# Three 16x8-head attention layers of a 12-layer decoder: first jobs, loads, splits and staging rearranged

## The reference, cut to what matters

```
h = layernorm(x)                      # per token, over 128 channels
q = (h @ Wq + bq) * scale             # the self layer has no q/k/v biases
k = src @ Wk + bk ; v = src @ Wv + bv # src: context (512 x 96), or h (256 x 128)
p = softmax(q_head @ k_head.T)        # 16 heads; L0 clamps the scores at 1e4
x = x + concat(p @ v_head) @ Wo + bo  # L3 regroups the heads before Wo
```

## Time and profile before

| | us |
|---|---|
| median of 3 executions | 2374.45 (2373.88 to 2378.79) |
| the profiled execution | 2378.78, its span 2377.0 |
| PE busy | 2000.3 (84% of the span) |
| PE weight load busy | 1195.5 (50%) |
| DVE busy | 1440.6 (61%) |
| ACT busy | 1108.8 (47%) |
| POOL busy | 647.4 (27%) |
| HBM | 46 GB/s over the span |

### The profile page before, as it was taken

The page is one execution under the profiler, slowest core; times in us unless marked ns, Lnnn a source line. Parts: engine busy times, 40 slices in busy tenths (PEclk is TensorE's granted clock), DMA queues, the critical chain, the costliest instruction groups (busy, mean ns, idle before and its releaser), DMA issues. The chain is left out here.

```text
span 2377.0 us, 37476 instructions
## 1 busy us (share of the span) xinstructions
PE 2000.3 (84%) x12495; PEld 1195.5 (50%) x12495; DVE 1440.6 (61%) x3369; ACT 1108.8 (47%) x2808; POOL 647.4 (27%) x907
## 2 busy tenths in 40 slices
PE   6679999879995887666999996656899999599997
PEld 3434544434442554544666664435566666244444
DVE  6468899444433554684777765562666665477762
ACT  4325555534431665333555553220566666167762
POOL 7434342100003432101111105301434432333312
PEclk9769999889995888887999998865999999689996
DMA  1133321386642330001000001101000000434321
GB/s 34 30 95 70 76 51 42 74 189 144 143 99 69 80 77 19 23 0 37 1 2 1 2 2 31 33 1 42 1 2 2 1 2 1 105 77 86 76 48 26
DMA packets 126321, 112.29 MB, mean 47 GB/s; under 512 B 61193, under 2 KB 98996, under 8 KB 123828
## 3 DMA queue, kind: packets, MB, share of 16 engines
q1 hardware_dynamic: 92852, 108.84, 19.8%
q10 hardware_dynamic: 33280, 1.05, 0.7%
HBM read 93.67 MB, written 15.20 MB: 46 GB/s over the span
## 5 line engine op out<-in xcount | busy, mean ns | idle before, releaser
L957 DVE TENSOR_REDUCE L_xattn_mx<-L_xattn_psS 128x1 f32<-128x512 f32 x512 | 326.2, 683 | 116.1 <-PE L_xattn_psS L1082 112.1
L1192 ACT ACTIVATE L_xattn_PT<-L_xattn_psT 128x512 f32<-128x512 f32 x512 | 283.2, 600 | 95.1 <-PE L_xattn_psT L1094 89.5
L603 ACT ACTIVATE L_attn_pr<-L_attn_psS,L_attn_negm 128x256 f32<-128x256 f32 (+1 forms) x512 | 222.0, 446 | 103.1 <-DVE L_attn_negm L403 68.0
L1082 PE MATMUL L_xattn_psS<-L_xattn_KR,L_xattn_QR 72*128 72x512 bf16 x512 | 212.8, 421 | 43.2 <-DVE L_xattn_mx L957 21.1
L401 DVE TENSOR_REDUCE L_attn_mx<-L_attn_psS 128x2 f32<-128x512 f32 x256 | 164.9, 686 | 114.3 <-PE L_attn_psS L512 114.2
L1094 PE MATMUL L_xattn_psT<-L_xattn_QR,L_xattn_KR 75*128 75x256 bf16 x1024 | 198.3, 279 | 3.8 <-ACT L_xattn_PT L1192 1.6
L1108 PE MATMUL L_xattn_psO<-L_xattn_PT,L_xattn_V 128*32 128x256 f32 x2048 | 193.1, 400 | 3.2 <-ACT L_xattn_PT L1192 1.1
L2068 DVE TENSOR_TENSOR L_ffn_act<-L_ffn_act,L_ffn_cwb 128x512 f32<-128x512 f32 x128 | 86.7, 690 | 129.9 <-ACT L_ffn_act L2198 106.0
L512 PE MATMUL L_attn_psS<-L_attn_qk 64*128 64x256 f32 x1024 | 146.6, 404 | 11.6 <-ACT L_attn_pr L603 11.6
L2133 PE MATMUL L_ffn_psU<-L_ffn_hT,L_ffn_wup 128*128 128x512 f32 x256 | 133.3, 612 | 13.6 <-ACT L_ffn_act L2198 13.6
L2198 ACT ACTIVATE L_ffn_act<-L_ffn_psU 128x512 f32<-128x512 f32 (+1 forms) x132 | 78.5, 597 | 135.7 <-PE L_ffn_psU L2133 131.8
(11 more groups left out here) (553 smaller groups left out, 3952.1 us busy)
## 6 DMA issues: line engine op xcount, KB each, us to landing
L_ffn_cwb<-L_ffn_weights_by_expert SPq DMA_DIRECT2D x64, 512.0 KB, 7.8
L_xattn_KR<-L_xattn_k_parts SPq DMA_DIRECT2D x96, 192.0 KB
L_xattn_QR<-L_xattn_q_parts SPq DMA_DIRECT2D x32, 288.0 KB
L_xattn_k_parts<-L_xattn_ks SPq DMA_DIRECT2D x48, 128.0 KB, 2.4
L_xattn_ctxT<-in_ctx SPq DMA_DIRECT2D x24, 192.0 KB, 2.4
L_attn_QR<-L_attn_q_parts SPq DMA_DIRECT2D x16, 288.0 KB
L_attn_KR<-L_attn_k_parts SPq DMA_DIRECT2D x48, 96.0 KB
L_xattn_q_parts<-L_xattn_qs SPq DMA_DIRECT2D x48, 64.0 KB, 2.1
```

Source lines behind the costliest of these rows:

```text
L603: ins = nc.scalar.activation(pr[n % 3][:, r, t, 0:width], psS[(2 * n + r) % 3][:, t, 0:width], ACT.Exp, bias=negm[:, n % 4, t, r:r + 1], s ...
L957: nc.vector.reduce_max(mx[:, b % 2, u, hd:hd + 1], psS[n % 2][:], AX.X).then_inc(s_used, 1)
L1082: ins = nc.tensor.matmul(psS[n % 2][:, i * keys:(i + 1) * keys], QR[b % NB][0:PAIR, hd, t * P:(t + 1) * P], KR[b % NB][0:PAIR, hd, :], sta ...
L1192: nc.scalar.activation(PT[n % NPT][:, 2 * u:2 * u + 2], psT[i % NPS][:], ACT.Exp).then_inc(exp_ready, 1)
```

## The change

All in layer_attention_heads8, but for one packed input.

- First jobs: T, Q and K of batch 0 write to banks of their own (psT[0], psT[1], psS[0]) and don't wait for psM; the reads follow.
- Loads: the biases bq and bk are packed into two more columns of the query weight (made on the host), so that qk_loaded counts two DMAs; wv is loaded before bv, both behind the query weight; the ones rows are loaded behind spread 0, and POOL makes the ones tile behind the second norm.
- Cross layers: V of batch 0 moves from step FIRST to FIRST + 1 (ahead of K of batch 1, behind the first scores); DVE_SPLITS 2 becomes 1.
- Two buffers each for qs and ks, with a staging semaphore each; ACT, splits and spreads wait for the batch two before.
- Self layer: EARLY 6 becomes 4, APART 7 becomes 9, BACK 8 becomes 9; T, Q, K, V at 0, 4, 6, 8. T, Q, K, V of batch 1 are then at -17, -13, -11, -9 (before -17, -15, -13, -11), of batch 2 at -8, -4, -2, 0 (before -10, -8, -6, -4), of batch 3 at 1, 5, 7, 9 (before -3, -1, 1, 3); modulo 16 later: M 7, A 9, O 10, T 12, M 15, Q 0, K 2, V 4. SP's order becomes stage 0, spread 0, ones rows, stage 1, spread 1, rows(0,0), rows(0,1), stage 2, spread 2, rows(1,0), stage 3, spread 3, rows(1,1), and as before from there.
- LAST: two empty steps fewer in L0, one step more in the self layer.

```
-    LEAD, PREP, STAGE, EARLY, DVE_SPLITS = (HH + 6, 38, 7, 3, 2) if from_ctx else (HH + 10, 52, 9, 6, 3)
+    LEAD, PREP, STAGE, EARLY, DVE_SPLITS = (HH + 6, 38, 7, 3, 1) if from_ctx else (HH + 10, 52, 9, 4, 3)
-    APART, BACK = (4, 6) if from_ctx else (7, 8)
+    APART, BACK = (4, 6) if from_ctx else (9, 9)
-    FIRST, LAST = -LEAD, NH + (16 if head_major else 10)
+    FIRST, LAST = -LEAD, NH + (16 if head_major else BACK + 2)
-        for i, kind in ((0, "K"), (2, "T"), (3, "Q")) if from_ctx else ((0, "T"), (2, "Q"), (4, "K")):
+        for i, kind in ((0, "K"), (2, "T"), (3, "Q")) if from_ctx else ((0, "T"), (4, "Q"), (6, "K")):
-        jobs[max(H * b - LATE_V, FIRST) if from_ctx else at + 6 * (b > 0)].append(("V", b, 0))
+        jobs[max(H * b - LATE_V, FIRST + 1) if from_ctx else at + 8 * (b > 0)].append(("V", b, 0))
-        qs, ks = sb("qs", [P, PARTS, S], BF16), sb("ks", [P, PARTS, keys], BF16)
+        qs, ks = ([sb(f"{n}{i}", [P, PARTS, w], BF16) for i in range(2)] for n, w in (("qs", S), ("ks", keys)))
+        q_staged, k_staged = ([sem(f"{v}_staged{i}") for i in range(2)] for v in "qk")
-        WQK, WV = (4, 2) if bq is not None else (2, 1)
+        WQK, WV = (2, 2) if bq is not None else (2, 1)
+        def bank_of(job):
+            kind, b, _ = job
+            if b == 0 and kind in "TQ":
+                return psT["TQ".index(kind)][:].rearrange("p k s -> p (k s)")
+            return psS[0][:] if b == 0 and kind == "K" else psM[:]
-            loads = [(wk_s[:], m.dram[wk], qk_loaded), (wq_s[:], m.dram[wq], qk_loaded)]
+            loads = [(wk_s[:], m.dram[wk], qk_loaded), (wqb[:], m.dram[wq if bq is None else f"{pre}_q_pack"], qk_loaded), (wv_s[:], m.dram[wv], v_loaded)]
             if bq is not None:
-                loads += [(bk_s[:], ...), (bq_s[:], ...), (bv_s[:], ...)]
-            loads += [(wv_s[:], m.dram[wv], v_loaded), (wo_s[:], ...), (bo_s[:], ...)]
+                loads += [(bv_s[:], rows(m.dram[bv]).to_broadcast((P, D)), v_loaded)]
+            loads += [ (wo_s[:], ...), (bo_s[:], ...)]
-            sp.wait_ge(ones_set, 1)
-            for i in range(NB):
-                sp.dma_start(KR[i][PAIR:PAIR + PARTS], ones[:]).then_inc(rows_set, 16)
+            def one_rows():
+                sp.wait_ge(ones_set, 1)
+                for i in range(NB):
+                    sp.dma_start(KR[i][PAIR:PAIR + PARTS], ones[:]).then_inc(rows_set, 16)
...
                     if kind == "spread":
                         spread(b)
+                        if b == 0:
+                            one_rows()
...
             link(nc.gpsimd.memset(eps[:], LN_EPS))
-            nc.gpsimd.memset(ones[:], 1.0).then_inc(ones_set, 1)
             norm(0)
+            pool.wait_ge(h_ready, TB)
             nc.gpsimd.memset(V[0][:], 1.0).then_inc(v_set, 1)
             norm(1)
+            pool.wait_ge(h_ready, 2 * TB)
+            nc.gpsimd.memset(ones[:], 1.0).then_inc(ones_set, 1)
...
-                wait(pe, psM_read, place[job])
+                bank = bank_of(job)
+                if not (b == 0 and kind in "TQK"):
+                    wait(pe, psM_read, place[job])
...
-                    wait(act, staged, 16 * PARTS * b)
-                    nc.scalar.activation(parts[:, 0], psM[:, 0:width], ACT.Identity, bias=add, scale=by).then_inc(psM_read, 1)
+                    wait(act, staged, 16 * PARTS * (b // 2))
+                    nc.scalar.activation(parts[:, 0], bank_of(job)[:, 0:width], ACT.Identity, bias=add, scale=by).then_inc(psM_read, 1)
```

More of the change, by code:

```diff
@@ L698, in layer_attention_heads8 @@
         sb, ps, sem = allocators(nc, es, pre)
-        wq_s, wk_s, wv_s, wo_s = sb("wq", [P, D]), sb("wk", [CK, D]), sb("wv", [CK, D]), sb("wo", [P, D])
-        bq_s, bk_s = sb("bq", [P, 1]), sb("bk", [P, 1])
+        wqb, wk_s, wv_s, wo_s = sb("wq", [P, D + 2 * (bq is not None)]), sb("wk", [CK, D]), sb("wv", [CK, D]), sb("wo", [P, D])
+        wq_s = wqb[:, 0:D]
+        bq_s, bk_s = (wqb[:, D + i:D + i + 1] if bq is not None else None for i in range(2))
         bv_s, bo_s = sb("bv", [P, D]), sb("bo", [P, D])
@@ L803, in spread_k @@
                 def spread_k(heads, done):
[L804 removed]
+                    sp.wait_ge(k_staged[b % 2], 16 * PARTS * (b // 2 + 1))
                     for i in range(PARTS):
@@ L855, in split_q @@
             eng.wait_ge(q_high, b + 1)
-            wait(eng, q_staged, 16 * PARTS * b)
-            split(eng, link, qf, qs, q_split)
+            wait(eng, q_staged[b % 2], 16 * PARTS * (b // 2))
+            split(eng, link, qf, qs[b % 2], q_split)
         def split_k(eng, link, b):
             eng.wait_ge(k_high, b + 1)
-            wait(eng, k_staged, 16 * PARTS * b)
-            split(eng, link, kf, ks, k_split)
+            wait(eng, k_staged[b % 2], 16 * PARTS * (b // 2))
+            split(eng, link, kf, ks[b % 2], k_split)
         @block.gpsimd
@@ L1050, in run @@
                     pe.wait_ge(o_loaded, 16 * 2)
-                wait(pe, psM_read, place[job])
+                bank = bank_of(job)
+                if not (b == 0 and kind in "TQK"):
+                    wait(pe, psM_read, place[job])
                 if kind == "Q":
-                    ins = nc.tensor.matmul(psM[:, 0:S], wq_s[:], hT[:], start=True, stop=True)
+                    ins = nc.tensor.matmul(bank[:, 0:S], wq_s, hT[:], start=True, stop=True)
                 elif kind == "K":
-                    ins = nc.tensor.matmul(psM[:, 0:keys], wk_s[:], kv_source(b), start=True, stop=True)
+                    ins = nc.tensor.matmul(bank[:, 0:keys], wk_s[:], kv_source(b), start=True, stop=True)
                 elif kind == "V":
@@ L1066, in run @@
                     for t in range(TB):
-                        ins = nc.tensor.transpose(psM[:, t * P:(t + 1) * P], h[:, t], m.ident[:])
+                        ins = nc.tensor.transpose(bank[:, t * P:(t + 1) * P], h[:, t], m.ident[:])
                 else:
@@ L1144, in read @@
                 if kind == "T":
-                    nc.scalar.copy(hT[:], psM[:, 0:S]).then_inc(psM_read, 1)
+                    nc.scalar.copy(hT[:], bank_of(job)[:, 0:S]).then_inc(psM_read, 1)
                 elif kind == "A":
@@ L1158, in read @@
                     whole, parts, width, staged, split_sem, high, bias, by = (
-                        (qf, qs, S, q_staged, q_split, q_high, bq_s, scale) if kind == "Q" else (kf, ks, keys, k_staged, k_split, k_high, bk_s, 1.0))
-                    add = bias[:] if bq is not None else 0.0
+                        (qf, qs[b % 2], S, q_staged[b % 2], q_split, q_high, bq_s, scale) if kind == "Q" else (kf, ks[b % 2], keys, k_staged[b % 2], k_split, k_high, bk_s, 1.0))
+                    add = bias if bq is not None else 0.0
                     wait(act, split_sem, SPLITS * b)
-                    nc.scalar.activation(whole[:], psM[:, 0:width], ACT.Identity, bias=add, scale=by)
-                    wait(act, staged, 16 * PARTS * b)
-                    nc.scalar.activation(parts[:, 0], psM[:, 0:width], ACT.Identity, bias=add, scale=by).then_inc(psM_read, 1)
+                    nc.scalar.activation(whole[:], bank_of(job)[:, 0:width], ACT.Identity, bias=add, scale=by)
+                    wait(act, staged, 16 * PARTS * (b // 2))
+                    nc.scalar.activation(parts[:, 0], bank_of(job)[:, 0:width], ACT.Identity, bias=add, scale=by).then_inc(psM_read, 1)
                     await_read(act, job)
@@ L2930 @@
         extra(f"{pre}_pack", np.concatenate([part("Wq").T, with_bias("Wk", "bk"), column("bq"), with_bias("Wv", "bv"), part("Wo")] + blank, 1))
+    for pre, q, bias_q, bias_k in (("L0_xattn", "Wq", "bq", "bk"), ("L3_xattn", "q_w", "q_b", "v_b")):
+        given = lambda v: arrays[f"in_{pre}_{v}"]
+        extra(f"{pre}_q_pack", np.concatenate([given(q), given(bias_q)[:, None], given(bias_k)[:, None]], 1))
     cos, sin = rotary_tables(S, 64)
```

16 lines of the change are left out of this document (7 added, 9 removed).

## The result

The changed kernel takes 2356.35 us (median of 5 executions, 2352.43 to 2362.3), the kernel before 2375.67 (2373.88 to 2383.59) beside it: ratio 0.9913, 95% interval 0.989 to 0.9937. The forecast was 2354. The profiled execution took 2356.35 with a span of 2354.5, against 2378.78 and 2377.0.

The account below looks back on a forecast made before the run. Bound: PE waiting on the load chain at starts, DVE's maxima in lead-ins, then PE itself except for late max rows. Cross 6.2 plus self 14.5 gives 20.7 off 2378.78; against the median, 2354 us, range 2345 to 2367.

Parts of the forecast that it names:

- the first four cases: Outcomes counted as faster: forecast 0.52, SP takes the stall 0.18, no early stalls 0.13, cross layers gain nothing 0.08; given 0.90.
- Cross start: Start of each cross layer: earlier loads, own banks and later ones rows bring first scores 2.3 us earlier.
- Cross lead-in: Cross layers, first scores to step 0: moved V0 and moved splits together gain 0.8 us per layer.
- (d): Cross lead-in: V0 behind the first scores, ahead of K1, puts the third maximum at 6.8 instead of 6.0; 0.8 us lost.
- (e): Cross lead-in: without Q1's split on DVE, the gap between maxima falls from 2.0 to 0.4 us; 1.6 gained.
- Self start: Start of the self layer: K0 freed earlier, mostly hidden by six stage DMAs on SP; 0.5 us gained.
- Self lead-in: Self layer, first scores to first turned scores: 31.9 us becomes 23.5, with batch 1 staged earlier; 8.4 gained.
- T3 and Q3 behind step 0, and two early stalls: Self layer after step 0: 1.4 us lost to jobs moved there, 1.8 lost to two early stalls on late max rows.
- GpSimd's delay and the small waits: Self layer after step 0: two later stalls from GpSimd's late max split go, 7.3 us; about eight small waits go, 1.5.
- SP takes the stall over: Rival, chance 0.18: self layer max rows land 5.7 us after issue, the 7.3 is not gained; 2361 to 2362 us.
- a sign that it is wrong: Self layer: ACT at L1153 waiting over 1 us for max rows in most batches would show the prediction wrong.
- Third layer: The second cross layer, started like the first, was forecast to gain the same 3.1 us.

Follow-up runs that it names:

- changed, again: A second trace of the changed kernel with nothing edited: 2356.23 us, ratio 0.9928 to the kernel before.
- e6: Changed kernel with the ones memset and ones DMAs back ahead of stage 0 in all three layers: 2354.03 us, ratio 0.9925.
- e4: Changed kernel with V of batch 0 back in step FIRST in the cross layers: 2349.32 us, ratio 0.9882.
- e1: Kernel before with only the two buffers each for qs and ks added: 2377.24 us, ratio 1.0003.
- e2: Kernel before with only the self layer's new steps, one buffer for parts: 2358.64 us, ratio 0.9935.
- e11: Kernel before with only EARLY 4 and APART 9 in the self layer: 2373.92 us, ratio 0.9984.
- e8: Changed kernel with two buffers for the split maxima (mp): 2354.11 us, ratio 0.9906.
- e10: Changed kernel with V0 at FIRST, two split-max buffers and stage and spread 3 later, but one buffer for parts: 2348.23 us, ratio 0.9894.

## Why the prediction was right, and where it was not

The total of the three layers, 20.7 forecast and 20.5 in the profiles, is right; several terms under it were not, and they offset one another. That it agrees within 0.2 is luck: with "changed, again" the same three layers give 22.8. (Of the chances, the first four cases add to 0.91, not 0.90.)

**Cross start, 2.3 each.** In the first cross layer four traces with the old start have 21.3 to 22.8 us, eight of nine with the new one (e6 aside) 19.7 to 20.2: 2.3, as forecast; the profiled execution itself had 0.1. In the third it is 2.9. The working was off inside: the spread went out 2.9 earlier, and 0.6 of it is not seen at the first scores. That the ones rows hold up the stores behind them, e6 shows (1.7 at the spread).

**Cross lead-in, 0.8 each.** Measured 1.5 and about 0.8, but V0's step (d) costs 3.2, not 0.8, and the splits (e) bring 4.7, not 1.6. What failed is the comparison "before: third maximum 6.0 after; now 6.8". Those 6.0 held K1's split on DVE, which another edit of the same change removed. With it removed the third maximum could stand at 3.2 (e4), and V0 puts it at 6.4. So the 0.8 was a sum of two edits, V0's cost less what K1's split gives, entered as V0's price. The sum was near; the price was not, and it called nearly harmless an edit that costs 6.8 us in two layers. The 6.4 itself was walked well.

**Self start, -0.5.** It did not come: 17.5 to 18.3 in kernels with the new start, 17.5 to 18.1 with the old. As feared, SP's six staging DMAs hide K's gain: ACT has K's first part ready 7.6 us after the layer's start instead of 8.8, but SP, which stages Q first, issues K's first store at 9.1 (before 8.9).

**Self lead-in, -8.4.** Measured -9.2, steps as walked (Q2's wait gone, M(0,0) at 10.9 for 11.4, step 0 at 22.7 for 23.5). That the gain is SP's order and not the buffer, as the walk had it with both at hand, e1 and e2 show: 2.3 against 9.2.

**T3 and Q3 behind step 0, and two early stalls, +3.2.** From step 0 to step 31, before and then after:

```profile
771.83:812.84 41.01, 35.85 (x285) 21.77 (x283) 24.84 (x49) 26.59 (x58) 19.66 (x34) 0.85 0.30 79
...
758.30:800.94 42.64, 35.08 (x286) 21.99 (x284) 24.53 (x53) 25.43 (x57) 19.02 (x33) 0.83 0.35 84
```

That is 1.6 lost (0.7 in "changed, again"). e11's 4.1 does not isolate this term, since its stall at step 3 comes from the single buffer. The place was half right: at step 15 PE waits 1.2 for ACT, and at step 24 it waits 4.0, not 1.6 to 1.8, and by another way: turned scores of batch 1's second half wait for rows(1,1) themselves. Stage(3) and spread(3), 9.7 us of SP, stood in the queue between the split and its rows. Four steps took 10.57 us, not 8.2.

**GpSimd's delay and the small waits, -7.3 and -1.5.** Sum 8.8; from step 31 to the layer's end 5.5 is gained (117.8 to 112.3; 6.1 in "changed, again"). e2 against e11 gives 8.8 too, but 3.4 of that lie before step 31: that agreement is chance. GpSimd's delay did go, and the two stalls behind it shrank, steps 39 and 55 from 8.17 and 8.6 us to 5.51 and 5.17. What the sum had at nothing is step 71: 4.9 us before, 7.61 now, because rows that stand right behind stage and spread come late there too. The stalls had been priced by windows (7.3) and not by their bare length (3.5). The Trainium skill ("TensorE: Matmul & The Clock Gate", section "What's actually happening") says that the array is held at half clock by default and activity releases it; the runs agree: at nearly the same wait at step 72 the changed kernel's four steps take 7.61 us at a granted clock of 0.78, those of e8 5.24 at 1.00.

**SP takes the stall over.** The rival's mechanism is true and its price was not. SP's chain at M(b,0) is 4.6 us to the end of its rows and 8.6 for stage and spread as walked, but rows sent right behind a spread release ACT 5.0 to 6.4 us after their first issue, not 3.4: 785.90 to 791.4 above, and in the next batches too (4.5 to 5.9 in "changed, again"). The 3.4 was read where GpSimd had held the rows back until the spread had drained. ACT waits over 1 us at M in five of the eight batches (4.49, 1.12, 1.04, 1.90, 3.61), which the prediction had named as a sign that it is wrong, and there the sign was right. With A two steps behind M this costs PE 0.4 at most through psM; what it does cost are the 9.6 us in which turned scores wait for the same rows. e8 lessens that from step 39 on, where four steps with A and O take 4.27, 4.19, 5.24 and 7.70 instead of 5.51, 5.17, 7.61 and 9.30.

**Third layer.** It gained 6.0, 3.7 of them up to step 0. The other 2.4 lie behind step 0, where kernels with the new cross layers have 254.9 to 259.9 us and those with the old 256.8 to 258.6. The ranges overlap and no run isolates it: open.

## What to carry to other kernels

Price each edit of a joint change with all the others held still. Against the kernel before or against the changed one, V0's step costs 3.2 us; only where one walk with two edits in it was set against the kernel before did it look nearly free, because another edit removed work at the same place. When a producer is made earlier, look at what stands in the DMA issuer's queue between it and its use, and take landing times from DMAs with the same neighbours ahead of them. A second buffer paid here only where the order of the queue used it (e10), and not in two orders that did not (e1, e2).

## What the hardware did unexpectedly

Landings depend on what is queued ahead of them. Stores of Q's parts land in 2.0 to 2.1 us without the ones rows ahead of them and in 2.5 to 2.9 with them. Whether DMAs queued behind matter as well is not shown: the ranges in e6 overlap, and the one wait of 6.5 us (issued 116.23, first scores 122.72) is explained by no run. Max rows need 3.3 to 3.5 us from the first issue to the release of ACT when the spread ahead has drained, and 4.4 to 6.4 when they are issued right behind it.

A wait of PE costs its length or much more, and the granted clock tells which. At step 72 PE waits 1.22 us in e8 and 1.38 in the changed kernel. In e8 the clock stays at 1.00, and the four steps take 5.24 us. In the changed kernel it falls in that stretch (0.78 on average), and they take 7.61: the same 43 matmuls are busy 5.78 us instead of 4.02. So 2.4 us for 0.16 more of waiting, 1.8 of it in the matmuls themselves. At step 24, 3.97 us of waiting at 0.68 makes 10.57, where a stretch without a wait takes 4.00. Why one short wait is followed by a fall of the clock and the other is not, these runs do not show.
